# A macaron block on one Trainium2 core: where v's and the output's row-paired matmuls change rows, and how the first layer's steps lie between the scores

## What is computed

```
x = x + 0.5 * ffn(layernorm(x))
x = x + attention(layernorm(x))       # 16 heads of 16 features, softmax over 2048 keys
x = x + 0.5 * ffn(layernorm(x))       # the same weights again

ffn(h): h = concat([h, -h]);  h = s0 * (h @ sign(k0));  h = 2 * relu(h)      # 512 -> 1024
        h = s1 * (h @ sign(k1));  h = 2 * relu(h)                            # 1024 -> 1024
        return s2 * (h @ sign(k2))                                           # 1024 -> 256
attention(x): q, k, v = x @ wq + bq, x @ wk + bk, x @ wv + bv
        att = softmax(q @ k.T / sqrt(16)) @ v;  return att @ wo.T + bo
```

## Time and profile before

| | |
|---|---|
| median of three runs | 1535.05 us |
| the profiled execution, device time | 1535.96 us |
| its span | 1532.1 us |
| PE busy (a modelled figure) | 1512.4 us, 99% |
| ACT busy | 1131.3 us, 74% |
| DVE busy | 584.7 us, 38% |
| chain that ended last | PE 98%, DVE 1% |
| attention steps | 278.8 to 1449 us of the span |
| granted TensorE clock | full speed throughout |

### The profile page before, as it was taken

How to read it: one execution, slowest core, us unless ns; L and a number is a source line. 1 busy time by engine, 2 the same in 40 slices (tenths; PEclk the granted TensorE clock), 3 DMA queues, 4 the chain that set the end, 5 groups by cost and what they waited for, 6 DMA issues and landing times.

```text
span 1532.1 us, 31536 instructions
## 1 busy us (share of the span) xinstructions
PE 1512.4 (99%) x12441; PEld 600.0 (39%) x12441; DVE 584.7 (38%) x1329; ACT 1131.3 (74%) x1655; POOL 59.9 (4%) x65
## 2 busy tenths in 40 slices
PE   6999999999999999999999999999999999999999
PEld 3555455333333433433333333334334334333354
DVE  6556746511431252325332242232332323332372
ACT  3212221798898898888989888988988988998721
POOL 2010111000000010010010000000000000000000
PEclk9999999999999999999999999999999999999999
DMA  4231223212231331223212113112212211311110
GB/s 124 49 90 35 80 79 103 80 50 74 74 67 44 104 105 48 54 96 95 80 52 81 53 40 107 39 39 67 80 39 67 80 39 53 105 48 33 36 42 16
DMA packets 110515, 101.44 MB, mean 66 GB/s; under 512 B 56224, under 2 KB 95904, under 8 KB 110368
## 3 DMA queue, kind: packets, MB, share of 16 engines
q1 hardware_dynamic: 109392, 98.86, 22.5%
q10 hardware_dynamic: 976, 0.53, 0.1%
HBM read 61.87 MB, written 25.43 MB: 57 GB/s over the span
## 4 chain that ended last, share of the span: by engine, by line
PE 98%; DVE 1%; POOL 0%; DMA 0%; ACT 0%; issue 0%; SPq 0%; POOLq 0%; DVEq 0%
PE psum L811 31%; PE psum L775 29%; PE psum L795 16%; PE psum L678 12%; PE psum L690 3%; PE psum L666 3%; PE psum L697 2%; PE psum L711 1%; POOL square L1079 0%; DMA x_sb<-in_x 0%; PE psum L704 0%; DVE xn L1002 0%; PE psum L654 0%; ACT prob L867 0%; DVE h_lo L911 0%
## 5 line engine op out<-in xcount | busy, mean ns | idle before, releaser
L867 ACT ACTIVATE prob<-psum 128x512 f32<-128x512 f32 (+1 forms) x1440 | 1018.7, 783 | 122.5 <-PE psum L795 116.9
L811 PE MATMUL psum<-prob,v_sb 128*17 128x512 f32 x4096 | 490.2, 595 | 0.0
L795 PE MATMUL psum<-q_st,k_st 64*128 64x512 f16 x2048 | 350.1, 379 | 1.5 <-ACT prob L867 0.9
L840 ACT ACTIVATE h_hi<-psum 128x512 f16<-128x512 f32 x183 | 110.0, 604 | 217.2 <-PE psum L678 161.5
L909 DVE TENSOR_SCALAR h_hi<-psum 128x512 f16<-128x512 f32 x73 | 50.5, 692 | 431.2 <-PE psum L775 431.1
L911 DVE SCALAR_TENSOR_TENSOR h_lo<-psum,h_hi 128x512 f16<-128x512 f32 x256 | 168.5, 687 | 82.3 <-ACT h_hi L840 79.8
L811 PEld LDWEIGHTS psum<-prob,v_sb 128*17 128x17 f32 x4096 | 96.6, 96 | 261.3 <-issue 164.2
L795 PEld LDWEIGHTS psum<-q_st,k_st 64*128 64x128 f16 x2048 | 82.8, 94 | 279.5 <-ACT prob L867 209.3
L775 PE MATMUL psum<-h_hi,w 64*128 64x512 f16 x1184 | 151.9, 376 | 0.3 <-DVE h_lo L911 0.3
L775 PE MATMUL psum<-h_lo,w 64*128 64x512 f16 x1184 | 151.8, 376 | 0.0
L678 PE MATMUL psum<-h_hi,w 128*128 128x512 f16 x432 | 102.1, 379 | 0.0
(11 more groups left out here) (101 smaller groups left out, 870.8 us busy)
## 6 DMA issues: line engine op xcount, KB each, us to landing
k_st<-k_halves SPq DMA_DIRECT2D x64, 512.0 KB, 4.4
q_halves<-piece SPq DMA_DIRECT2D x32, 256.0 KB, 2.5
q_st<-q_halves SPq DMA_DIRECT2D x64, 128.0 KB, 4.9
x_rows<-x_sb SPq DMA_DIRECT2D x16, 256.0 KB, 2.2
k_halves<-piece SPq DMA_DIRECT2D x16, 256.0 KB, 2.9
att_rows<-o_sb SPq DMA_DIRECT2D x128, 32.0 KB
x_sb<-x_rows SPq DMA_DIRECT2D x8, 512.0 KB, 4.0
att_t<-att_rows SPq DMA_DIRECT2D x16, 256.0 KB
```

The source lines that it names most:

```text
L795: mm = pe.matmul(psum[:, score_bank[h + r], :], k_st[rows, slot, t * P:(t + 1) * P], q_st[rows, slot, :], start=True, stop=True)
L811: mm = pe.matmul(psum[32 * j:32 * j + va, O_BANK, :], v_sb[:, b * key_tiles + t, GROUP * g4 + j, :], prob[:, h % PROBS, :], start=(t == 0) ...
L840: act.activation(hi, psum[:, bank, :], ACT.Relu).then_inc(act_done, 1)
L867: act.activation(prob[:, to:to + count, :], psum[:, bank:bank + count, :], ACT.Exp, scale=score_scale / QK_SCALE ** 2).then_inc(exp_sem, 1)
```

## The change

Three edits. (1) For v and out the row swap is no longer done once for each of the two 256-column parts, but once for the bank: first all four slots on the first rows (both parts), then all four on the others. The accumulation's start flag is given once for each bank. (2) In steps whose side work is l1, one pair of scores stands ahead of the first four slots instead of two, and two pairs stand between the two fours instead of one. (3) In those steps the exponentials are taken one bank at a time, all but the last two, where before up to three activations took two banks each. The idle work of a step (loads, fetches, norms) is also listed ahead of the first scores instead of behind them; it runs on other engines than the scores.

```diff
--- before.py
+++ after.py
@@ -296,19 +296,25 @@
     for n in range(att_steps):
         work.append(Step("att", n))
         lay_scores(n)
-        work.append(Step("score", n, 0))
         lay_idle(n)
+
+        first_layer = side[0].kind == "l1"
+        pairs = (1, 3, 4) if first_layer else (2, 3, 4)
+        work.append(Step("score", n, lo=0, hi=pairs[0]))
         if side[0].kind != "l2":
             lay_long(math.inf)
         elif side[0].hi + sum(PAIRS["l2"]) < 2 * FILLS["l2"][0]:
             lay_long(1.0)
         for between, slots in enumerate(PAIRS[side[0].kind]):
             lay_pair(slots)
-            work.append(Step("score", n, 1 + between))
+            work.append(Step("score", n, lo=pairs[between], hi=pairs[between + 1]))
         if columns and not side[0].n:
 
-            lay_exps(n, ((0, 1), (1, 2), (3, 1), (4, 1), (5, 2), (7, 1)))
+            lay_exps(n, ((0, 1), (1, 1), (2, 1), (3, 1), (4, 1), (5, 1), (6, 2)) if first_layer else
+                     ((0, 1), (1, 2), (3, 1), (4, 1), (5, 2), (7, 1)))
             lay_column(columns.pop(0))
+        elif first_layer:
+            lay_exps(n, ((0, 1), (1, 1), (2, 1), (3, 1), (4, 1), (5, 1), (6, 2)))
         else:
             lay_exps(n, ((0, 1), (1, 2), (3, 2), (5, 2), (7, 1)))
         if n:
@@ -365,7 +371,7 @@
     for s in work:
         if s.mate and s.last():
             changes_before[s.mm] = changes
-            changes += 4 if s.kind in ("l3", "v", "out") else 2
+            changes += 4 if s.kind == "l3" else 2
 
 
 
@@ -625,7 +631,7 @@
                 if s.kind == "att":
                     pe_attention(s.u)
                 elif s.kind == "score":
-                    for pair in ((0, 1), (2,), (3,))[s.m]:
+                    for pair in range(s.lo, s.hi):
                         pe_scores(s.u, pair)
                 elif s.kind == "values":
                     pe_values(s.u)
@@ -734,15 +740,19 @@
                     if bank.free_dve:
                         pe.wait_ge(dve_done, bank.free_dve)
 
-            wide = s.kind in ("l3", "v", "out")
-            length = n // 2 if wide else n
+
+
+            length = n // 2 if s.kind == "l3" else n
             for i in range(s.lo, s.hi):
-                part, turned = (i // (2 * length), i // length % 2) if wide else (0, i // length)
+                part, turned = (i // (2 * length), i // length % 2) if s.kind == "l3" else (0, i // length)
                 j = i % length
                 if turned and j == 0:
 
                     pe.wait_ge(halves, changes_before[s.mm] + 2 * (part + 1))
                 term, k = divmod(j, length // 2) if s.kind in ("l1", "l2", "l3") else (0, j)
+                column = part
+                if s.kind in ("v", "out"):
+                    column, k = divmod(j, kd)
                 if not turned:
                     if s.kind == "l1" and s.m == 0 and i == 0:
                         pe.wait_ge(flipped, 16 * (flip_no[u, 0 if u < blocks else 2] + 1))
@@ -768,9 +778,9 @@
                     elif s.kind == "qk":
                         w, a = (wq_sb, wk_sb)[m % 2][rows, k, m // 2 * P:(m // 2 + 1) * P], at[rows, k, :]
                     else:
-                        tile = m * per_bank + part
+                        tile = m * per_bank + column
                         src, wide_w = {"l3": ((h1_hi, h1_lo)[term], w2), "v": (at, wv_sb), "out": (att_t, wo_sb)}[s.kind]
-                        to = psum[:, bank.bank, part * dim:(part + 1) * dim]
+                        to = psum[:, bank.bank, column * dim:(column + 1) * dim]
                         w, a = src[rows, k, tile * P:(tile + 1) * P], wide_w[rows, k, :]
                     mm = pe.matmul(to, w, a, start=(turned == 0 and j == 0), stop=(turned == 1 and j == length - 1))
                     if i == 2 * n - 1:
@@ -826,7 +836,7 @@
             for s in steps:
                 u, m, bank = s.u, s.m, s.bank
                 if s.kind == "score":
-                    act_exps(s.u, (0, 4, 6)[s.m], (4, 6, 8)[s.m])
+                    act_exps(s.u, 2 * s.lo, 2 * s.hi)
                 elif s.kind == "w1":
                     act_w1()
                 elif not s.on_act or s.kind not in FILLS or not s.last():
```

## The result

The changed kernel took 1538.76 us (median of 12 runs, 1538.08 to 1539.68) where the kernel before took 1535.24 (12 runs, 1534.84 to 1536.2) beside it: 3.5 us longer, ratio 1.0023 with a 95% interval of 1.0015 to 1.0031. Forecast were 1.75 us longer, 1536.8, with a range of 1533.0 to 1539.6. The sign was as written and the losses stand in the steps that were named; one term of the sum was a third too small.

A forecast was written before the change was run, and what follows sets the result against it. TensorE was taken to bound the attention. Gains of 3.3 and 1.45 us against losses of 3.4 + 0.7 + 2.4 = 6.5 us gave 1.75 us longer, 1536.8 us, with a range of 1533.0 to 1539.6.

The forecast's parts named there:

- v and out: In 22 v and out steps the swap's wait of 0.15 us each goes: 3.3 us gained.
- the rival of the rows that keep costing: Float32 weights stay exposed at borders of turned slots, 2.1 to 2.2 us of gain missing: 1538.9 us; 6%.
- The l1 swap: In each of 36 l1 steps the swap's wait goes, 0.05 us; 1.45 us counted for the 29 without a column.
- The l1 bank: In 20 l1 steps behind an l1 step without a column, late banks delay the first slot 0.17 us: 3.4 us lost.
- the faster rival: Late banks in l1 and l2 steps stay hidden, only the gains of 5.1 us are left: 1529.9 us; 14%.
- The column: In seven l1 steps, sq or range matmuls wait for the fourth exponential, net 0.10 us each: 0.7 us lost.
- From l1 to l2: In l2 steps behind l1 runs, second scores wait for the last two banks, 0.30 us in eight places: 2.4 us lost.
- The slower rival, slow releases: Banks release 0.10 us slower at each of 28 first l1 slots and l2 scores: 2.8 us more, 1539.6 us; 14%.
- no change that can be measured: The whole kernel stays within about 0.2%, 3.1 us, of the kernel before; 62%.
- the case that had 23%: The whole kernel becomes slower by more than about 0.2%, 3.1 us; 23%.

The follow-up runs named there:

- the half alone: Only the single row swap of v and out, l1 steps as in the kernel before: 1531.99 us, ratio 0.9978 against the kernel before.
- the last two apart: The changed kernel with the last two banks of each l1 step taken one at a time: 1535.64 us, ratio 1.0001 against the kernel before.
- both edits: The changed kernel with the last two banks taken one at a time and `h_hi` ahead of the sixth exponential: 1531.61 us, ratio 0.9975 against the kernel before.
- the old pairs: The changed kernel with the l1 steps' scores in their old order, one-bank exponentials kept: 1535.97 us, ratio 1.0005 against the kernel before.

## Why the prediction was right, and where a term was mis-sized

*v and out: right.* 3.19 us in 22 steps, 0.12 to 0.16 each, for 22 × 0.15; the first step of a v pair lasts 4.65, for the 4.62 forecast, and three out steps that were long before stay at 4.69 and 4.74, where the forecast had 4.54 for every out step. The wait moved to a place 1263.68 - (1260.22 + 1.03) = 2.4 us after what it waits for, and the rival of the rows that keep costing fell with it, in the changed kernel and in the half alone.

*The l1 swap: right,* 0.05 us a step: the nine steps without a new wait lost 0.45 us.

*The l1 bank: right.* `h_hi` at 3.43 in a run's first step and 3.61 in the later ones, the last lo at 4.10 in a run's first step, the slot 0.18 late where 0.17 was forecast, in the 20 steps named. Moving `h_hi` alone removed it, so the chain from the second scores through ScalarE to VectorE is shown, and the faster rival (late banks are hidden) is out.

*The column: right in the sum, in part by luck.* The seven steps grew by 0.10 us in the mean, as forecast, but by -0.05 to 0.16 one by one. The sq matmul begins 2.81 us after its step's first scores in four of them, for the 2.84 forecast, at 2.85 in the step with the range, and in two at 2.70, not late at all. One of these two lasts 4.85 us here and 4.99 in the kernel with the last two apart, with the same order of its instructions, so part of these figures is not the wait for the fourth exponential. The old order and grouping in these seven steps took the 0.10 away.

*From l1 to l2: the mis-sized term.* I wrote "The scores come at 5.01 to 5.09 instead of 4.76: 0.25 to 0.33, I take 0.30" and counted eight places, 2.4 us. Measured were 3.71, and this is 1.31 of the 1.67 us by which the sum was short. Three parts. The scores came 0.36 us late and not 0.30. The exponential took 1.07 us and not the 1.02 of rows 10: that row does not stand behind an `h_hi`, and the two-bank exponentials that do took 1.07 in the kernel before too (median of 59). And the release took 0.14. The low end of the term, 5.01, stands for a release of 5.01 - 4.94 = 0.07 us, and no run shows one: of all scores in the traces before and after none follows the exponential that frees its bank by less than 0.144 us. Behind the late scores the slots lost 0.02 us more in four of the eight places and 0.11 to 0.18 in the others. That their own waits, queued behind the scores that stall, cost this is argued and not shown; three of the four places are those that keep 0.12 us with both edits, where no scores stall, so most of it may hang on the place in the program, as above. And the ninth place, which I had counted at nothing, lost 0.08, by the slots' wait for the last lo that the kernel with the last two apart shows in all nine. That the two-bank exponential carries most of the term is shown by that same kernel, which leaves 0.87 us of it.

*The slower rival, slow releases.* In part. Its price was 0.10 us more at each of 28 places; the releases at these places took 0.14 to 0.15, as rows 9 and 10 had them, so its mechanism didn't hold. But its point, 0.05 us more per place, was passed, by (3.42 - 1.75)/28 = 0.06, most of it in nine places and for the reasons above. So the measured time is nearer to this rival's than to the forecast. The same is true of the chances: the forecast read "no change that can be measured", within 3.1 us or 0.2%, with 62%. Measured were 3.5 us, 0.23% (0.15 to 0.31%): by its middle the case that had 23%. The time lies inside the range because the range reached up to this rival.

## What to carry to other kernels

When a wait is moved, follow not only what it waits for but what the move delays: a pair of scores four slots later held up an exponential, through it the `h_hi` queued behind, VectorE's last product, and a bank that two engines share. A change in halves should be timed in halves: here one gained 3.2 us and the other lost 6.6. And where an engine works through a queue without slack, look first at the instruction that another engine waits for: `h_hi` one place forward was worth 3.5 us, at no more work.

## What the runs showed of the hardware

- A stall of TensorE cost more than its own length here. The scores of the l2 step stood until 0.14 us after the exponential, and the slots behind them followed after 0.24 to 0.39 us instead of 0.22. A late lo did the same: 0.27 us to the slot in an l2 step, 0.15 in an l1 step. Further waits queued behind the first may be why; no run separates them.
- A two-bank exponential directly behind an `h_hi` takes longer to its end: 1.07 us (median of 59, in the kernel before and after; up to 1.10 with the old pairs) against 1.02, which is what it takes behind another exponential (median of 528 and of 486) and after a wait alike. A release must be read from a row with the same instruction ahead of it.
- Up to 0.15 us of a step hung on the place of its code in TensorE's program, and came and went with 8 or 20 instructions added ahead of step 8 (one run each).
